# A Mamba-2 block between two small feed-forwards on one core: a new order of work in the chunked scan, and the scan's output kept in PSUM

## The reference, cut to what matters

```python
x = x + 0.5 * ffn(layernorm(x))          # dequantised 512x512 weight, LoRA, bias
n = layernorm(x); h = n + mamba2(rmsnorm(n)); x = x + h + mlp(rmsnorm(h))
x = x + 0.5 * ffn(layernorm(x))

# mamba2, 4 heads of 128, state 128, chunks of 128 tokens (16 chunks)
z, xs, Bs, Cs, dt = split(x @ w_in.T)
xs, Bs, Cs = silu(conv4(xs, Bs, Cs) + conv_b)            # four taps along the tokens
cs  = cumsum(softplus(dt) * A)                             # inside a chunk
att = (C @ B.T) * exp(cs_q - cs_k) * (k <= q)              # "scores" S
y   = att @ (x * dt) + exp(cs) * (C @ state)               # scan output of a chunk
state = exp(cs_end) * state + (B * decay * dt).T @ x       # state update
y   = (y + D * x) * silu(z);  out = y @ w_out.T
```

## Time and profile before

| what | value |
|---|---|
| runs | 781.28, 782.09, 782.08 us; median 782.08 |
| profiled execution | 783.73 us, of which the span from the first to the last instruction is 782.0 us |
| mean granted TensorE clock | 0.985 |
| busy PE / PEld | 748.5 us (96%) / 364.4 us (47%) |
| busy DVE / ACT / POOL | 642.9 us (82%) / 458.2 us (59%) / 352.8 us (45%) |

### The profile page before, as it was taken

One profiled execution on the slowest core, in us unless ns is written; L12 is line 12 of the kernel. 1 busy time (PEld: TensorE's weight loads), 2 busy tenths in 40 slices (PEclk: granted clock), 3 DMA queues, 4 the chain that ended last, 5 costly groups with the idle time before them and its releaser, 6 DMA issues.

```text
span 782.0 us, 10656 instructions
## 1 busy us (share of the span) xinstructions
PE 748.5 (96%) x3424; PEld 364.4 (47%) x3424; DVE 642.9 (82%) x1245; ACT 458.2 (59%) x895; POOL 352.8 (45%) x403
## 2 busy tenths in 40 slices
PE   8999997999899789799999999999999999999998
PEld 3444554555455445354444444444444444444444
DVE  7799998778768887996799988878779779657994
ACT  4868877587765666554536555645645555535451
POOL 5631646565453358866614125124224224223574
PEclk9999999999899899999999999999999999999999
DMA  8934645654421121524060554544544643444464
GB/s 299 186 74 80 167 95 105 138 114 90 83 64 41 41 55 40 128 48 95 14 148 15 103 123 79 140 81 81 139 84 75 148 82 68 76 81 66 105 178 142
DMA packets 98790, 77.67 MB, mean 99 GB/s; under 512 B 65600, under 2 KB 73088, under 8 KB 98736
## 3 DMA queue, kind: packets, MB, share of 16 engines
q0 software_dynamic: 17280, 31.46, 22.6%
q1 hardware_dynamic: 78592, 41.01, 19.9%
q10 hardware_dynamic: 2864, 4.52, 2.4%
HBM read 24.77 MB, written 5.54 MB: 39 GB/s over the span
## 4 chain that ended last, share of the span: by engine, by line
PE 63%; DVE 21%; ACT 8%; issue 4%; DMA 2%; POOL 2%; ACTq 0%; SPq 0%; DVEq 0%; POOLq 0%
PE PS L2123 57%; DVE raw L1578 3%; DVE stage L1578 2%; PE PS L2261 1%; DVE w_in L1682 1%; DVE state L1560 1%; DVE st L1399 1%; DMA x_t<-hb 1%; PE PS L2229 1%; PE PS L2253 1%; DVE h2n_p L1490 1%; DVE xs L1498 1%; ACT xds L922 1%; ACT pre L972 1%; DVE S L1534 1%
## 5 line engine op out<-in xcount | busy, mean ns | idle before, releaser
L2123 PE MATMUL PS<-h,w_in 128*128 128x512 f16 x480 | 111.5, 388 | 0.6 <-DMA h<-hn_p 0.5
L2123 PE MATMUL PS<-h,x_t 128*128 128x512 f16 x408 | 94.0, 379 | 1.7 <-DVE pre L1948 1.6
L773 POOL DMA_DIRECT2D xs<-x x42 | 36.4, 866 | 94.0 <-ACT x L1263 93.1
L2123 PEld LDWEIGHTS PS<-h,w_in 128*128 128x128 f16 x480 | 47.3, 100 | 65.4 <-issue 15.7
L2123 PE MATMUL PS<-n_T,stage 128*128 128x512 f16 x288 | 71.5, 379 | 0.0
L1263 ACT ACTIVATE x<-PS,d_d 128x512 f32<-128x512 f32 x59 | 40.3, 683 | 39.5 <-PE PS L2123 38.6
L2123 PEld LDWEIGHTS PS<-h,x_t 128*128 128x128 f16 x408 | 39.4, 98 | 50.2 <-issue 2.6
L576 POOL TENSOR_TENSOR r<-mv,mhalf 128x1 f32<-128x1 f32 (+1 forms) x32 | 29.4, 920 | 69.3 <-DVE mv L1403 53.0
L2123 PE MATMUL PS<-pre,stage 128*128 128x512 f16 x192 | 49.3, 379 | 0.0
L1233 ACT ACTIVATE xds<-tm,dgh 128x512 f32<-128x512 f32 x24 | 17.3, 722 | 53.3 <-DVE tm L2047 53.3
L2123 PEld LDWEIGHTS PS<-n_T,stage 128*128 128x128 f16 x288 | 28.2, 98 | 34.0 <-ACT x L1263 0.3
(11 more groups left out here) (352 smaller groups left out, 1910.6 us busy)
## 6 DMA issues: line engine op xcount, KB each, us to landing
xs<-x POOLq DMA_DIRECT2D x58, 256.0 KB, 3.3
xs<-n POOLq DMA_DIRECT2D x21, 256.0 KB, 3.3
xl<-x POOLq DMA_DIRECT2D x17, 256.0 KB, 3.3
x_t<-x_in SPq DMA_DIRECT2D x16, 256.0 KB, 3.1
x_t<-hb POOLq DMA_DIRECT2D x16, 256.0 KB, 3.8
out<-x_t SPq DMA_DIRECT2D x15, 256.0 KB, 2.3
raw_gu<-gate_t SPq DMA_DIRECT2D x7, 512.0 KB, 4.5
raw_gu<-up_t SPq DMA_DIRECT2D x7, 512.0 KB, 6.4
```

The lines of the kernel that those rows point to most:

```text
L773: po.dma_start(end_row(c), d_tmps[d % 3], accum_op=ALU.add).then_inc(s_acc[d % 3], 16)
L2123: ins = pe.matmul(out_, lhs(a, b, k), rhs(a, b, k), start=first and n == 0, stop=last and n == len(todo) - 1)
```

## The change

1. **All orders inside the scan are rewritten.** For chunks 8 to 15 `step` is replaced by `late_steps`, written out one by one, on DVE, ACT and POOL. In these, a step of DVE begins with `gate_y(c)` and `advance(c)`, and `weights(c+1)`, `scan1(c+1)` and `low_y(c)` stand ahead of most taps, silus and bound work; on ACT `scan_ecs`, `scan1`, `high_y` and `scan_decay` stand ahead of most convs and tanhs; on POOL the sums `t_op` are cut into pieces of two to four between `scan_c`, `scan_d` and `rms2`. For chunks 0 to 7 the order changes less: `conv` in steps with j = 1 moves ahead of `hi1`, some `slot_a` of ACT move by one place.
2. **y stays in PSUM.** `gate_y` reads PSUM and silu(z) and writes y back to the same PSUM bank; `high_y` (ACT) and `low_y` read it there.
3. **`low_y` runs on DVE in all sixteen chunks**, and twelve leave POOL. In chunks 0 to 7 it stands behind `scan1(c+1)` (or behind `lo0` where j = 2 and c = 7).
4. **s2_diag(c+1) waits for low_y(c)** in place of gate_y(c), as the bank is now read until then.
5. **Loads.** `load_pair(1)` is cut in two: gate and up (`load_gu(1)`) at the start of step 14 behind the first half of the weight cut (`cut_b_gu`), down (`load_d(1)`) at the end of step 14's list on SP, behind `t2(13)`.

```diff
-            return szs[(c // CH) % 2][:, :, cols], y_lo[...]
+            return sz, heads(B_YT), y_lo[...]
             def gate_y(c, j):
-                ve.scalar_tensor_tensor(y, heads(B_YT), d_ih[:, :], y, ALU.mult, ALU.mult)
+                ve.scalar_tensor_tensor(y, heads(B_YT), d_ih[:, :], sz, ALU.mult, ALU.mult)
             def s2_diag(c, j):
-                    pe.wait_ge(e_y, c)
+                    pe.wait_ge(e_y_lo, c)
             # SP
-                if c == 3 * CH + 1:
-                    sp_.wait_ge(e_w_gu1d, 2)
-                    load_pair(1)
+                if c == 3 * CH + 2:
+                    load_gu(1)
...
                 if c > 3 * CH:
                     t2(c - 1)
+                if c == 3 * CH + 2:
+                    load_d(1)
             # POOL
-                    if c not in LO_DVE:
-                        low_y(c)
+                scan_c(3 * CH, 0)
+                sums(0, 2)
+                scan_d(3 * CH, 0)
+                sums(2, 4)
+                rms2(2 * CH + 3, 3)
+                sums(4, 6)
+                scan_c(3 * CH + 1, 1)
+                scan_d(3 * CH + 1, 1)
+                sums(6, 10)
...
+                scan_d(3 * CH + 2, 2)
+                sums(12, 14)
+                rms2(3 * CH + 1, 1)
+                sums(14, 16)
+                scan_c(3 * CH + 3, 3)
+                scan_d(3 * CH + 3, 3)
             # ACT, steps 0 to 7
-                if j == 2 and i + 1 < NS:
+                if j in (1, 2):
                     slot_a(i + 1, SLOTS[j][0])
-                if a < NCH:
-                    hi1(a, a % CH)
+                hi1(a, a % CH)
             # DVE, steps 9, 10, 14 and 15
+                c = 2 * CH + 1
+                taps(3, 1, 3)
+                gate_y(c, 1)
+                advance(c, 1)
+                weights(c + 1, 2)
+                scan1(c + 1, 2)
+                low_y(c)
+                taps(3, 2, 6)
+                silu(3, 1)
+                silu(3, 2)
+                lo2(c - 1)
+                maximum_gu(1).then_inc(e_max, 1)
+                taps(3, 3, 9)
+                residual2(c, 1)
+                silu(3, 3)
+                c = 2 * CH + 2
+                gate_y(c, 2)
+                advance(c, 2)
+                bound_row(0)
+                low_y(c)
+                taps(3, 4, 12)
+                for k in range(15, 18):
+                    softplus(3, k)
+                weights(c + 1, 3)
+                scan1(c + 1, 3)
+                silu(3, 4)
+                scale_read(0)
...
+                c = 3 * CH + 2
+                gate_y(c, 2)
+                advance(c, 2)
+                low_y(c)
+                scan1(c + 1, 3)
+                lo2(c - 1)
+                bound_g(1, 0)
+                gate_up(0, 2)
+                residual2(c, 2)
+                bound_g(1, 1)
+                gate_lo(0, 2)
+                bounds(1)
+                c = 3 * CH + 3
+                gate_y(c, 3)
+                low_y(c)
+                t_los(1, 0, 1)
+                lo2(c - 1)
+                gate_up(0, 3)
```

More of the change, by code:

```diff
@@ L681, in step @@
                 a = c + 2 * CH
-                if a < NCH:
[L683 to L686, removed]
-                    if c not in LO_DVE:
-                        low_y(c)
-                    scan_d(c + 1, (c + 1) % CH)
+                ln1_chain(a, a % CH)
+                scan_c(c + 1, (c + 1) % CH)
+                scan_d(c + 1, (c + 1) % CH)
                 if a + 1 < NCH:
@@ L693, in step, with late_steps, sums @@
                     ln0(a + 2, (a + 2) % CH)
-                early_sums = c in (3 * CH, 3 * CH + 1)
-                if early_sums:
-                    sums(c)
                 rms2(c, c % CH)
[L698 to L704, removed]
+            def late_steps():
+                for c in range(2 * CH, 2 * CH + 3):
+                    scan_c(c + 1, (c + 1) % CH)
+                    scan_d(c + 1, (c + 1) % CH)
+                    rms2(c, c % CH)
+                scan_c(3 * CH, 0)
[7 more added lines that the diff above has]
+                sums(6, 10)
+                rms2(3 * CH, 0)
+                sums(10, 12)
+                scan_c(3 * CH + 2, 2)
+                scan_d(3 * CH + 2, 2)
[4 more added lines that the diff above has]
+                scan_d(3 * CH + 3, 3)
+                rms2(3 * CH + 2, 2)
+                sums(16, 20)
+                rms2(3 * CH + 3, 3)
+            def sums(first, end):
+                for n in range(first, end):
                     t_op(n // N_TOP, n % N_TOP)
             N_TOP = 8
-            T_EARLY = {2 * CH + 2: range(0, 3), 2 * CH + 3: range(3, 6), 3 * CH: range(6, 12),
-                       3 * CH + 1: range(12, 16), 3 * CH + 2: range(16, 20)}
             def t_ready(q, r_):
@@ L1018, in step @@
                 a = c + 2 * CH
[L1019 to L1028, removed]
+                i_late, late = (c - 1) // CH + 1, SLOTS[(c - 1) % CH][1:] if c > 0 else ()
+                scan_ecs(c + 1, (c + 1) % CH)
+                scan1(c + 1, (c + 1) % CH)
+                for q in late[1:]:
+                    slot_a(i_late, q)
+                if late:
                     slot_b(i_late, late[0])
-                if c not in HIGH_FIRST and c not in HIGH_LATE:
+                if c in HIGH_MID:
                     high_y(c)
@@ L1033, in step @@
                     hi0(a + 1, (a + 1) % CH)
[L1034 to L1037, removed]
+                for q in late[1:]:
+                    slot_b(i_late, q)
+                if c > 0:
                     hi2(c - 1, (c - 1) % CH)
-                if c + 1 < NCH:
-                    scan_decay(c + 1, (c + 1) % CH)
-                if c in HIGH_LATE:
+                scan_decay(c + 1, (c + 1) % CH)
@@ L1278, in _ @@
             prologue()
-            for c in range(NCH):
+            for c in range(2 * CH):
                 step(c)
+            late_steps()
             hi2(NCH - 1, CH - 1)
@@ L1892, in step @@
-                if c == 3 * CH:
-                    dn_lo(0)
-                    t_los(0, 3)
-                if c == 3 * CH + 1:
-                    bound_g(1, 0)
-                if c == 3 * CH + 2:
-                    gate_y(c + 1, j + 1)
-                    t_los(1, 0, 1, 2, 3)
-                if c == 3 * CH + 3:
-                    bound_row(1)
+                if j == 2:
+                    residual2(c, j)
+                slot_a(i + 1, SLOTS[j][0], {1: 9}.get(j))
+                if j == 0:
+                    softplus(i + 1, 0)
+                    softplus(i + 1, 1)
+                    softplus(i + 1, 2)
```

345 lines of the change are left out of this document (223 added, 122 removed).

## The result

The changed kernel takes 763.09 us (median; 761.47 to 766.01 in four runs). Its ratio to the kernel before is 0.9755, 95% interval 0.9713 to 0.9797: 19.2 us less of 782.1, with some 3 us to either side. The forecast was 765.6 us, its range 754 to 777. The profiled execution took 761.71 us, span 760.0, mean granted clock 0.998 (before 0.985). In the experiments too the gain is one minus the ratio to the kernel before, measured on the same chip, times 782.1.

What follows compares the result with a forecast made beforehand. TensorE's passage through the chunk loop was taken as the bound, losing 35.7 us to waits and clock. Terms that stay sum to 19.2 us, so the gain is 16.5: 782.1 - 16.5 = 765.6 us, range 754 to 777.

Steps and rivals of the forecast that it cites:

- the second bound: Behind the loop: bound_row(1), last in its list, costs 1.0 us at bound_spread(1).
- The bound: TensorE's loop over the chunks sets the end, one for one; the loop loses 35.7 us to waits and clock.
- y in PSUM: VectorE, all chunks: each low_y takes 0.68 us; gate_y's write to PSUM costs 0, at most 1.6 us in all.
- w(2), w(6): TensorE in steps 2 and 6: waits of 1.2 and 1.0 us for low_y stay, and the clock holds.
- Steps 3 and 4, scores of 8: f(11) and f(12) find their banks not yet read, 1.8 us; the scores of chunk 8 cost 0.3 us.
- Steps 9 and 10: The 4.98 us wait goes; VectorE's backlog costs 4.0 us in step 10: spread 0.7, csm 0.7, scale_read 1.4, taps 1.2.
- Steps 11 to 15: Waits of 2.9 and 4.4 us go; scores of chunks 14 and 15 come 1.8 and 1.9 us late.
- The load: Pair 1's load_d(1) behind t2(13): VectorE stands 4.8 us at bound_g(1, 0); TensorE waits 4.3 us plus 1.9 of clock.
- A: Rival: nearly all waits in the loop go, 5 of the 19.2 us stay, 751 us; chance 0.17.
- B: Rival: only the first eight chunks gain, 9 us, the late half stays as it is, 773 us; chance 0.18.
- C: Rival: slower, VectorE and POOL collide in steps 9 to 15 at 0.97 us each; 22 collisions give 787 us; chance 0.09.
- D: Rival: nothing to be seen, waits only change names, gains and costs equal within 1.6 us; chance 0.04.

Runs made afterwards that it cites:

- e_sbuf_dve: Changed kernel with y back in SBUF in place of silu(z) and s2_diag waiting for gate_y; low_y stays on VectorE in all chunks; 767.76 us.
- e_y_only: Kernel before with only y in PSUM, low_y on VectorE in all chunks and s2_diag waiting for low_y; every order as before; 770.76 us.
- e_both_lo2: e_both with lo2(6) of step 7 moved behind scan1(8) in VectorE's list; 756.58 us.
- e_load: Changed kernel with load_d(1) right behind load_gu(1) in SP's list, ahead of t2(13); 757.11 us.
- e_both: Changed kernel with the edits of e_load and e_bound together; 755.76 us.
- e_three: e_both with POOL's sums 10 and 11 behind scan_d(14) in place of ahead of scan_c(14); 757.75 us.
- e_four: e_both with POOL's sums 10 and 11 behind scan_d(14), 12 to 15 behind scan_d(15), and ScalarE's t_hi(1, 1 to 3) at the end of step 14; 755.83 us.
- e_bound: Changed kernel with bound_row(0) ahead of gate_y(10) and scale_read(0) ahead of weights(11) in VectorE's list; 761.34 us.

## Why the prediction was right, and where its steps were wrong

The predicted sum was a gain of 16.5 us with 19.2 us of loss staying. Measured: 19.2 us of gain, 22.0 between the two profiled executions, and 15.1 us staying. So by the trace what stays was put 4.1 us too high, mostly at w(2) and w(6), the scores of chunk 15 and the second bound; that 765.6 us lies only 2.5 us above the measured median is in part luck. By its steps:

- **The bound.** Right: all but the 0.9 us ahead of it came out of the loop, one for one, and nothing behind it moved.
- **y in PSUM.** Right in both prices: 0.68 us for each `low_y` (0.67 to 0.69), under 0.01 us for the write. The Trainium skill's rule (GPSIMD Engine Reference, Specifications) held for `low_y`: 2.93 us with two SBUF operands beside POOL's sums, 0.68 with one in PSUM. But the prediction's remark that the stretched rows are just those with two SBUF inputs is too narrow: the softplus instruction of 1.24 us reads one SBUF tensor and a constant. The other figure that was weighed (the Trainium skill, VectorE: DVE Perf Modes, section on the TRN2 errata) would make a `low_y` from PSUM longer than one from SBUF. The runs don't show it: medians of 673 and 678 ns from PSUM, and 676 and 680 ns from SBUF in the early half of `e_sbuf_dve`, where nothing stretches them.
- **w(2), w(6).** Predicted 1.2 and 1.0 us, measured 0.17 and 0.27; with the old order 0.9 and 0.9. The price was good for the old order. The sum left out that the new order brings VectorE to `low_y(2)` 2.1 us sooner (39.0 us after diag 0, in `e_y_only` 41.2). The moved convs are the likely reason, but no run moves them alone. At w(5), which the prediction put at no wait within 0.3 us, TensorE waited 0.43.
- **Steps 3 and 4, scores of 8.** Predicted 1.8 and 0.3, measured 0.9 and 1.3. `e_both_lo2` shows that more than its place in the list makes chunk 8 late.
- **Steps 9 and 10.** The total was right (4.0 against 3.8 us), the split was not: 2.7 at the spread of the bound, 1.1 for `scale_read`, next to nothing at `csm`. Half of the 2.0 us missed at the spread is that `bound_row(0)` ends in an instruction on 3x3 elements that lay beside `scan_c`: 1.20 us in place of 0.22. The rest is its place behind the backlog, `gate_y(10)` and `advance(10)`. The VectorE and POOL rows are

```profile
250.82 0.27 DVE L1721 TENSOR_REDUCE mr<-PS 3x1 f32<-3x128 f32 x1
251.13 1.20 DVE L1722 TENSOR_SCALAR mdg<-ident,mr 3x3 f32<-3x3 f32 x1
```

```profile
250.77 1.53 POOL L608 TENSOR_TENSOR stage<-stage,ecs 128x512 f32<-128x512 f32 x1
```

- **Steps 11 to 15.** The 2.9 and 4.4 us went. The scores of chunk 14 were right (1.8 predicted, 2.1 measured), those of 15 too dear (1.9 against 0.4), and `bound_spread(1)` costs nothing (1.0). As VectorE's wait for the load stands behind `scan1(15)` in the list, it doesn't delay those scores.
- **The load.** Right: 4.8 us predicted and 5.20 measured on VectorE, 4.3 + 1.9 against 4.0 + 1.7 on TensorE; `e_load` gives 6.0 back. A nearest row for the landing (3.1 us) and the queue's order were enough.
- **What was wrong behind a right total is the attribution.** The prediction gave the late waits of 4.98, 2.94 and 4.42 us to the order alone. `e_y_only` has none of the new orders and loses only 2.25, 2.35 and 2.75 there: in steps 8 and 9 because POOL's `low_y` no longer holds VectorE up, in chunks 11 and 13 because `low_y`, on VectorE before and after, reads PSUM and is not stretched. The prediction gave the 2.82 us of `low_y(13)` as a row and put no gain on it. The order then removes what is left, and the place of the load costs 5.7 us of it.

Of the rivals, A (nearly all waits go) describes the kernel that the load should have left: `e_both` is at 755.8 us, and rival A's 751 was not reached. B (only the early half) is refuted by the trace: of 22.0 us between the profiled times 11.6 lie ahead of diag 8 and 10.4 behind. C (VectorE and POOL in each other's way) is real as a mechanism, 1 us and more for a collision, but the change made fewer of them (VectorE rows in the loop over 0.25 us longer than others of their form: about 26 before, 19 after); it shows in `e_three` and `e_sbuf_dve`. D is out.

Not settled: how the 12.4 us of `e_y_only` part between the operand in PSUM and the engine, which only the new order was tested for, and what, besides the collision of `weights(8)`, keeps the scores of chunk 8 late. The best of the versions, `e_both` and `e_four`, can't be told from each other at this resolution; both beat the changed kernel, by 7 to 8 us.

## What to carry to other kernels

When an engine shares SBUF access with another, count what an instruction costs beside it, not alone: with one operand in PSUM all sixteen subtractions took 0.67 to 0.69 us and held POOL up no more, and the same two moves sped up steps whose order nobody had touched. When a DMA issue is put behind another wait in its queue, ask who waits for the data and whether that same engine produces what the queue waits for; here one line was worth 6 us of the 25. And mend waits in the order of time and read the trace again after each: the next one is often the same backlog at another place.

## What the runs showed that was not expected

Tiny instructions are held up beside POOL like big ones, and by more than their own size: 3x3 elements took 1.20 in place of 0.22 us, 128x16 took 1.24 in place of 0.17, and `weights` with 128x4 took 2.09 in place of 0.16 us in the changed kernel (VectorE, step 13):

```profile
294.38 2.09 DVE L1630 TENSOR_TENSOR wv<-Ld,dt 128x4 f32<-128x4 f32 x1 [0.86 <-ACT Ld L929]
```

It seems to wait for the rest of POOL's work, not for its own share of the traffic: the three end at 252.33, 252.22 and 296.47 us, and the POOL instructions beside them at 252.30, 252.19 and 296.45. In return instructions of VectorE hold POOL up: the `affine_select` takes 0.64 us alone, 1.02 and 1.62 beside `low_y` with y in SBUF, and 1.69 in `e_both_lo2`.

Of TensorE's clock: the wait of 3.95 us cost 1.7 us behind it, that of 3.35 us at the same place in `e_bound` 2.7 us (24 matmuls in 8.05), and that of 2.72 us nothing (the next 24 in 5.35). The 2.1 us for the scores of chunk 14 cost nothing in the changed kernel, and in `e_bound` the two matmuls behind it took 2.08 in place of 1.12 us. So the length of a wait alone doesn't tell its price in this range.
